# Self-attention of a three-part decoder block: scores and the product with V as plain float32 products on halves of the array

## The chip, the cores and the metric

The kernel runs on one core of one Trainium2 chip. The metric is the time on the device in microseconds (us), the median over runs of the whole program. Engines are named as in the profile: PE is TensorE (matmuls), PEld its weight loads, DVE is VectorE, ACT is ScalarE, POOL is GpSimd, SP is SyncE, which here only issues DMAs.

## The reference

The input x has 16 batches of 128 tokens with 256 features. Three residual blocks follow one another, each on a layernorm of x. Only the first is touched here.

```
x = x + attn(layernorm(x))      # 16 heads of 64, over the 128 tokens of a batch
x = x + xattn(layernorm(x))     # 16 heads of 16, keys and values from ctx, masked
x = x + ffn(layernorm(x))       # 8 experts of 512, gelu, one gate per token

Q, K, V = einsum('btd,hkd->bthk', x, W) + b         # for each of the three
scores  = einsum('bqhk,bshk->bhqs', Q, K) / sqrt(64)
out_h   = einsum('bhqs,bshk->bqhk', softmax(scores), V)
result  = einsum('bqhk,hdk->bqd', out_h, W_O) + b_O
```

## The kernel before

All data are float32. Most matmuls run as three products of values that are split in two parts (`three`, L718): each operand is a rounded high part (type fp32r) and a low part, the rest that rounding left, and high x high, high x low and low x high are summed in PSUM. Every operand that goes into such a product is therefore written twice, mostly the high part by ACT and the low part by DVE or POOL.

The 16 batches form four groups of four (512 tokens). Phase 0 is self-attention of the four groups, phase 1 the cross attention, phase 2 the experts. In phase 0 the 16 heads are taken in 8 chunks of two heads, and each chunk in two slots. A slot holds one "quad": two heads x two batches, four 128x128 score tiles side by side in one PSUM bank (S0 or S1, by turns). 16 slots make a group. Each slot also does one sixteenth of what the group needs beside it: one projection of Q or K for two heads and all 512 tokens (bank A0), one of V for one batch and four heads (left half of bank A1), and half of a chunk's output projection (banks Y0 and Y1). A slot on PE is: scores (L821 to L835), output projection (L893), product with V (`probs_v`, L845), transposes of the probabilities (L841), V projection, Q or K projection.

The life of one quad in phase 0:
- PE: scores from Q (split in two) and K (split in two, laid out with the other head's rows zero, so that one matmul of 256 columns gives two heads), 6 matmuls for two batches.
- DVE: negated row maximum (L1329). ACT: four exponentials with their row sums (L1138). DVE: reciprocal (L1334). POOL: normalise (L1593).
- PE: four transposes into bank T (L841). ACT: the high part of the transposed probabilities (L1149). DVE: the low part (L1224, tile PT).
- PE: product with V. For each of four tiles a matmul of the high probabilities with both parts of V side by side (L860, 128 columns of weights) and one of the low ones with the high part of V (L863, 64 columns). Both parts' results stand in different partitions of bank O.
- ACT: copies one half of O (L1156). DVE: adds both halves and the bias (L1352). POOL: splits the result in high (L1609) and low (L1615). PE: output projection.

The order of the work on each engine is written out in tables, `PE_ORDER`, `ACT_ORDER`, `DVE_ORDER`, `POOL_ORDER` (L511 to L568): for each kind of slot a list of steps with a lag in slots. The product with V, for example, lags two slots behind the scores in phase 0. `steps` (L329) turns a slot's number into the steps' arguments, `run` (L410) walks the table. Engines wait for each other by semaphores only. Each of the banks A0, T and O and each half of A1 has one buffer: what fills it next waits until the last reader is done.

At the seam to phase 1, keys and queries of the cross attention make a round trip by DMA through DRAM (`first_keys`, `first_stack`, `first_queries`) before its first scores (L821, L833). In phase 1 the product with V (L873) is already a plain float32 product: lhs and rhs have type float32, are not split, and four heads stand in four groups of 32 output partitions.

## Time and profile before

| what | value |
|---|---|
| median of 3 runs | 878.22 us (877.76 to 878.98) |
| the profiled execution, its own time | 878.83 us |
| its span, first to last instruction | 877.0 us |
| mean granted TensorE clock | 0.992 |
| busy: PE, PEld, DVE, ACT, POOL | 837.7, 747.4, 536.3, 597.8, 303.6 us |
| phase 0, first to last scores of self-attention | 16.4 to 325.6 us |
| phase 1, first scores to last product with V | 331.7 to 503.4 us |

The busy time of PE counts a matmul from its start to the modelled end of its drain, and neighbours overlap, so a busy PE isn't PE at its peak, and a matmul's own duration isn't what it costs. What a sequence of matmuls costs is read from the distance between the starts of one sequence and of the next. In the timeline, equal instructions in a row are merged into one line with their count, and a bracket at the end says how long the engine stood idle before it and for whom.

### The profile page before, as it was taken

The page shows a single profiled execution, that of the slowest core. Times are in us where ns is not written, and L with a number is a line of the kernel's source. Part 1 is how long each engine was busy: PE and PEld are TensorE (multiplying, and loading weights), DVE is VectorE, ACT ScalarE, POOL GpSimd, SP SyncE. Part 2 cuts the span into 40 slices and gives each one's busy share as a digit, 9 for nine tenths or more (in the row PEclk, how much of TensorE's full clock was granted, in tenths as well). Part 3 has the DMA queues.
Part 4 walks back from the last instruction along what each step waited for, and adds up shares of the span by engine and source line. Part 5 has one row for each costly group of instructions (what it writes and reads, how often), then busy time and mean ns, then how long its engine had stood idle before and what let it go on. Part 6 is the DMA issues. An engine that isn't in the chain of part 4 may idle for free.

```text
span 877.0 us, 17326 instructions
## 1 busy us (share of the span) xinstructions
PE 837.7 (96%) x6043; PEld 747.4 (85%) x6043; DVE 536.3 (61%) x1127; ACT 597.8 (68%) x1724; POOL 303.6 (35%) x350
## 2 busy tenths in 40 slices
PE   8999999999999996889887999999999999999998
PEld 7899989989998985677766689998999999999997
DVE  6898898889889876677767564543233322332223
ACT  5999888888888875878788757654544445444643
POOL 5575656445564665575755520000000000000000
PEclk9999999999999998999999899999999999999999
DMA  6220000000000036565564232300000000000000
GB/s 202 90 62 26 1 1 2 1 1 1 1 25 1 1 71 171 132 159 147 119 157 109 62 95 87 96 1 25 2 1 1 24 0 0 0 25 1 1 1 25
DMA packets 22894, 42.25 MB, mean 48 GB/s; under 512 B 3352, under 2 KB 3872, under 8 KB 22816
## 3 DMA queue, kind: packets, MB, share of 16 engines
q1 hardware_dynamic: 21936, 40.64, 17.5%
q8 instruction: 45, 0.74, 0.4%
q10 hardware_dynamic: 880, 0.60, 0.2%
q14 instruction: 33, 0.27, 0.1%
HBM read 30.35 MB, written 10.49 MB: 47 GB/s over the span
## 4 chain that ended last, share of the span: by engine, by line
PE 75%; DVE 11%; ACT 6%; issue 3%; DMA 2%; POOL 1%; SPq 1%; ACTq 0%; POOLq 0%
PE Y L721 26%; PE A L721 24%; PE S L721 15%; PE T L841 4%; ACT probs L1138 3%; PE O L860 2%; DVE arena L1300 2%; DVE nm L1329 2%; PE O L863 1%; DVE xn L1252 1%; DVE probs L1342 1%; DVE arena L1224 1%; DVE PT L1224 1%; DMA wst<-in_pieces 1%; PE S L821 1%
## 5 line engine op out<-in xcount | busy, mean ns | idle before, releaser
L1224 DVE TENSOR_TENSOR PT<-probs,PT 128x512 fp32r<-128x512 f32 x128 | 89.7, 700 | 227.6 <-ACT PT L1204 227.6
L721 PEld LDWEIGHTS Y<-arena,PT 128*128 128x128 f32 x1536 | 199.9, 191 | 11.4 <-DVE PT L1224 1.4
L721 PE MATMUL Y<-arena,PT 128*128 128x256 f32 x1536 | 203.9, 283 | 0.4
L1138 ACT ACTIVATE probs<-S,nm 128x128 f32<-128x128 f32 x512 | 181.7, 377 | 27.8 <-DVE nm L1329 26.4
L1593 POOL TENSOR_TENSOR probs<-probs,rinv 128x512 f32<-128x512 f32 x128 | 133.0, 1043 | 154.3 <-DVE rinv L1334 154.1
L721 PE MATMUL A<-XT,arena 128*128 128x512 f32 x612 | 160.9, 397 | 1.7 <-DVE arena L1300 0.7
L1204 ACT ACTIVATE PT<-probs 128x512 fp32r<-128x512 f32 x128 | 80.8, 631 | 103.0 <-PE Y L721 102.6
L721 PEld LDWEIGHTS A<-XT,arena 128*128 128x128 f32 x612 | 107.8, 189 | 23.4 <-DVE arena L1300 3.9
L1138 ACT ACTIVATION_READ_ACCUMULATOR probs<-S,nm 128x1 f32 x512 | 110.6, 216 | 0.0
L1329 DVE TENSOR_REDUCE nm<-S 128x4 f32<-128x512 f32 x128 | 87.4, 683 | 30.6 <-PE S L833 18.5
L721 PE MATMUL S<-XT,arena 128*128 128x512 f32 x384 | 99.7, 395 | 0.0
L841 PE MATMUL T<-ident,probs 128*128 128x128 f32 x512 | 80.4, 280 | 16.3 <-DVE probs L1342 14.9
L841 PEld LDWEIGHTS T<-ident,probs 128*128 128x128 f32 x512 | 56.7, 142 | 25.1 <-issue 19.3
L721 PEld LDWEIGHTS S<-XT,arena 128*128 128x128 f32 x384 | 68.0, 189 | 11.4
L1352 DVE SCALAR_TENSOR_TENSOR oraw<-O,bias,opart 64x256 f32<-64x256 f32 x128 | 61.0, 477 | 19.4 <-ACT opart L1156 17.6
L721 PE MATMUL Y<-arena 128*128 128x256 f32 x480 | 71.9, 287 | 0.3 <-POOL arena L1615 0.3
L1173 ACT ACTIVATE probs<-S,bias 128x512 f32<-128x512 f32 x64 | 43.7, 683 | 36.5 <-PE S L721 36.5
L1173 ACT ACTIVATE probs<-A,bias 128x512 f32<-128x512 f32 x64 | 43.7, 684 | 36.6 <-PE A L721 36.5
L1588 POOL TENSOR_TENSOR rstd<-ve,mhalf 128x4 f32<-128x4 f32 x12 | 12.6, 1048 | 158.0 <-DVE ve L1239 158.0
L721 PEld LDWEIGHTS Y<-arena 128*128 128x128 f32 x480 | 64.2, 194 | 1.3 <-POOL arena L1615 1.0
L1615 POOL TENSOR_TENSOR arena<-oraw,arena 128x256 fp32r<-128x256 f32 (+1 forms) x72 | 58.4, 811 | 5.2
L721 PEld LDWEIGHTS S<-arena 128*128 128x128 f32 x384 | 54.3, 189 | 5.7 <-DVE arena L1293 0.6
(137 smaller groups left out, 1375.9 us busy)
## 6 DMA issues: line engine op xcount, KB each, us to landing
wst<-in_pieces SPq DMA_DIRECT2D x43, 256.0 KB, 2.6
stage<-arena SPq DMA_DIRECT2D x32, 256.0 KB, 2.3
arena<-stage SPq DMA_DIRECT2D x51, 128.0 KB, 4.0
arena<-stage SPq DMA_DIRECT2D x21, 256.0 KB, 3.9
craw<-in_ctxT SPq DMA_DIRECT2D x4, 512.0 KB, 4.1
out<-craw SPq DMA_DIRECT2D x8, 256.0 KB, 2.3
xs<-in_x SPq DMA_DIRECT2D x3, 512.0 KB, 4.4
craw<-in_pieces SPq DMA_DIRECT2D x6, 256.0 KB, 2.8
```

What stands on the lines that cost most here:

```text
L721: mm = pe.matmul(acc, lhs[a], rhs[b], start=first and i == 0, stop=last and i == 2, skip_group_check=shared)
L841: mm = pe.transpose(T[:, u * P:(u + 1) * P], probs[:, ring(ph, g, n), u * P:(u + 1) * P], ident[:, :])
L860: pe.matmul(O[:, u * P:(u + 1) * P], v4.rearrange("p s c -> p (s c)"), PT[:, n % 2, 0, u * P:(u + 1) * P], start=True, stop=False, skip_gr ...
L1138: last = act.activation(probs[:, ring(ph, g, n), u * P:(u + 1) * P], S[n % 2][:, u * P:(u + 1) * P], ACT.Exp, bias=nm[:, n % 4, u:u + 1], ...
L1173: act.activation(hid(m), H[m % 4][:, :], ACT.Gelu, bias=bias[:, B1 + m:B1 + m + 1]).then_inc(act_done, 1)
L1204: act.activation(PT[:, m % 2, 0, :], hid(m), ACT.Copy).then_inc(h_hi, 1)
L1224: dve.tensor_tensor(out_, src, hi.bitcast(F32), ALU.subtract).then_inc(sem_, 1)
L1300: last = dve.scalar_tensor_tensor(K[rows_, c % 2, 1, :, h, :], bank[rows_, :].rearrange("p (b c) -> p b c", b=TILES), bias[rows_, BK1 + c: ...
L1329: dve.tensor_reduce(nm[:, n % 4, :], s3, axis=AX.X, op=ALU.max, negate=True).then_inc(maxed, 1)
L1352: last = dve.scalar_tensor_tensor(oraw[h * DH1:(h + 1) * DH1, n % 2, 0:256].rearrange("p (b c) -> p b c", b=2), o4[:, :, h, :], bias[0:DH1 ...
L1593: pool.tensor_tensor(p3, p3, rinv[:, n % 4, :].unsqueeze(2).to_broadcast([P, 4, P]), ALU.mult).then_inc(normed, 1)
L1615: pool.tensor_tensor(to[:, 1, :], raw, to[:, 0, :].bitcast(F32), ALU.subtract).then_inc(o_lo, 1)
```

## The change

Phase 0 only, and with it the order tables.

- Q, K, V and the transposed probabilities aren't split any more. Each is one float32 tile (`qkv`, and `probs` in place), written by one engine: K and V by ACT, Q by DVE, the transposed probabilities of even quads by ACT, of odd ones by DVE.
- Both slots of a chunk are scored in one go (`chunk_scores`): for four batches and two heads, 8 plain float32 matmuls of 128x128 with 64 rows of contraction. Head 0 stands in partitions 0 to 63 of Q and K and goes to bank S0, head 1 in partitions 64 to 127 and goes to S1.
- The product with V of a chunk is in one go too (`chunk_v`): 8 plain float32 matmuls, head 0 into partitions 0 to 63 of bank O, head 1 into 64 to 127.
- The result is taken from O by DVE in two instructions, high part with bias and low part with bias, straight into `AT`. ACT's copy, DVE's two sums and POOL's two splits of phase 0 go.
- The tables have new steps "even", "odd" and "cross". In phase 0 scores and product with V come once per two slots; transposes lag one quad, the product with V one chunk. A quad index now stands for one head and four batches. An evacuation of Q, K or V stands in the slot of its projection, not in the next one.
- The cross attention's tiles KP, QP, XA and the second context buffer have places of their own in the arena, so several waits at the seam go (in `split_context`, `blank_keys`, `qk_evac`, `part_hi`). `scores` and `probs_v` for phase 1 compute what they did.

```diff
...
-        V = region(4096).rearrange("p (r t h s c) -> p r t h s c", r=2, t=TILES, h=4, s=2)
-        K = region(4096).rearrange("p (r s b h c) -> p r s b h c", r=2, s=2, b=TILES, h=2)
-        Q = region(2048).rearrange("p (r s c) -> p r s c", r=2, s=2)
+        def halves_of(what, cols):
+            return cols.rearrange(f"p (s {what} t) -> p s {what} t", s=2, t=GT)
+        CT = [halves_of("k", region(2048)), halves_of("k", region(2048))]
+        XA = halves_of("k", region(2048))
+        KP = region(2048).rearrange("p (r s c) -> p r s c", r=2, s=2)
+        QP = region(2048).rearrange("p (r s c) -> p r s c", r=2, s=2)
         AT = region(2048).rearrange("p (r s c) -> p r s c", r=2, s=2)
...
+        qkv = sb("qkv", [P, 4096], F32)
+        V = qkv[:, 0:2048].rearrange("p (r t h c) -> p r t h c", r=2, t=TILES, h=4)
+        K = qkv[:, 2048:3072].rearrange("p (r c) -> p r c", r=2)
+        Q = qkv[:, 3072:4096].rearrange("p (r c) -> p r c", r=2)
...
-                return XT if g % 2 else CT[0]
+                return XT if g % 2 else PT
...
         PE_ORDER = (
-            (("scores", "quad", (0, 0)), ("proj", "proj", (4, 6)),
-             ("pv", "quad", (2, 5)), ("transpose", "quad", (1, 3)), ("xp", "xp", (0, 0)),
-             ("v", "v", (0, 0)), ("qk", "qk", (0, 0))),
+            (("xp", "xp", (0, 0)), ("v", "v", (0, 0)), ("transpose", "odd", (1, 0)), ("qk", "qk", (0, 0)),
+             ("scores", "even", (0, 0)), ("pv", "odd", (1, 0)), ("transpose", "even", (1, 0)),
+             ("proj", "proj", (3, 6))),
...
+            def chunk_scores(g, c):
+                pe.wait_ge(qk_lo, nth(QK_F1, 0, g, 2 * c + 1))
+                pe.wait_ge(exped, nth(SLOT_F2, 0, g, 2 * c - 1))
+                for b in range(TILES):
+                    at = slice(b * P, (b + 1) * P)
+                    for h in range(2):
+                        rows_ = slice(h * DH1, (h + 1) * DH1)
+                        mm = pe.matmul(S[h][:, at], Q[rows_, c % 2, at], K[rows_, c % 2, at],
+                                       start=True, stop=True)
+                        if b == TILES - 1:
+                            mm.then_inc(scores_ps, 1)
...
-                        b, h = 2 * (n % 2) + u // 2, u % 2
-                        v4 = V[:, cp % 2, b, 2 * (c % 2) + h, :, :]
-                        pe.matmul(O[:, u * P:(u + 1) * P], v4.rearrange("p s c -> p (s c)"),
-                                  PT[:, n % 2, 0, u * P:(u + 1) * P], start=True, stop=False,
-                                  skip_group_check=True)
-                        mm = pe.matmul(O[0:DH1, u * P:(u + 1) * P], v4[:, 0, :],
-                                       PT[:, n % 2, 1, u * P:(u + 1) * P], start=False, stop=True,
-                                       skip_group_check=True)
...
+            def chunk_v(g, c):
+                if c % 2 == 0:
+                    pe.wait_ge(v_lo, nth(VJ_F1, 0, g, 2 * c + 3))
+                pe.wait_ge(o_lo, nth(SPLIT_F2, 0, g, c - 1))
+                for b in range(TILES):
+                    for h in range(2):
+                        mm = pe.matmul(O[h * DH1:(h + 1) * DH1, b * P:(b + 1) * P],
+                                       V[:, c // 2 % 2, b, 2 * (c % 2) + h, :],
+                                       probs[:, ring(0, g, 2 * c + h), b * P:(b + 1) * P],
+                                       start=True, stop=True)
+                        if b == TILES - 1:
+                            mm.then_inc(pv_ps, 1)
...
+                    c = job // 2
+                    act.wait_ge(qk_ps, nth(QK, ph, g, job))
+                    act.activation(K[:, c % 2, :], bank_qk(ph, g, job)[:, :], ACT.Identity,
+                                   bias=bias[:, BK1 + c:BK1 + c + 1]).then_inc(qk_lo, 1)
+                    return
...
-            def probs_hi(ph, g, n):
-                if ph == 1 and n % 2 == 0:
-                    return
-                act.wait_ge(pt_ps, nth(SLOT_F4, ph, g, n))
-                if ph == 0:
-                    act.wait_ge(pv_ps, nth(SLOT_F2, ph, g, n - 2))
-                    act.activation(PT[:, n % 2, 0, :], T[:, :], ACT.Copy).then_inc(pt_hi, 1)
-                else:
+            def probs_copy(ph, g, n):
+                if ph == 0 or n % 2 == 1:
+                    act.wait_ge(pt_ps, nth(SLOT_F4, ph, g, n))
                     act.activation(probs[:, ring(ph, g, n), :], T[:, :], ACT.Copy).then_inc(pt_lo, 1)
-            def out_first(ph, g, n):
-                if ph == 0:
-                    act.wait_ge(pv_ps, nth(SLOT_F2, ph, g, n))
-                    act.activation(opart[DH1:P, :], O[DH1:P, :], ACT.Copy).then_inc(o_part, 1)
...
             def qk_low(ph, g, job):
+                    if job == 1 and opening(g):
+                        dve.wait_ge(ready_b, 2)
+                    c = job // 2
+                    dve.wait_ge(qk_ps, nth(QK, ph, g, job))
+                    dve.tensor_scalar(Q[:, c % 2, :], bank_qk(ph, g, job)[:, :], bias[:, BQ1 + c:BQ1 + c + 1],
+                                      None, ALU.add).then_inc(qk_lo, 1)
+                    return
...
-            def v_low(ph, g, job):
-                if ph == 0:
-                    dve.wait_ge(v_hi, nth(VJ, ph, g, 3 if opening(g) and job == 2 else job))
-                    r, t = job // 4 % 2, job % 4
-                    sub_lo(V[:, r, t, :, 1, :], acc_v(g, job).rearrange("p (h c) -> p h c", h=4),
-                           V[:, r, t, :, 0, :], v_lo)
...
+            def row_max(ph, g, quad):
+                for n in (quad, quad + 1) if ph == 0 else (quad,):
+                    dve.wait_ge(scores_ps, nth(SLOT, ph, g, n))
+                    s3 = S[n % 2][:, :].rearrange("p (u c) -> p u c", u=4)
+                    dve.tensor_reduce(nm[:, n % 4, :], s3, axis=AX.X, op=ALU.max, negate=True
+                                      ).then_inc(maxed, 1)
...
             def out_sum(ph, g, n):
-                c = n // 2
                 if ph == 0:
-                    dve.wait_ge(o_part, nth(PART, ph, g, n))
-                    dve.wait_ge(o_lo, nth(SPLIT_F2, ph, g, n - 2))
-                    o4 = O[0:DH1, :].rearrange("p (b h c) -> p b h c", b=2, h=2)
-                    p4 = opart[DH1:P, :].rearrange("p (b h c) -> p b h c", b=2, h=2)
-                    for h in range(2):
-                        last = dve.scalar_tensor_tensor(
-                            oraw[h * DH1:(h + 1) * DH1, n % 2, 0:256].rearrange("p (b c) -> p b c", b=2),
-                            o4[:, :, h, :], bias[0:DH1, BV1 + 2 * c + h:BV1 + 2 * c + h + 1],
-                            p4[:, :, h, :], ALU.add, ALU.add)
-                    last.then_inc(o_sum, 1)
+                    c = n // 2
+                    dve.wait_ge(pv_ps, nth(SLOT_F2, ph, g, n))
+                    dve.wait_ge(oproj, nth(OPROJ, ph, g, c - 2))
+                    dve.tensor_scalar(AT[:, c % 2, 0, :], O[:, :], bias[:, BV1 + c:BV1 + c + 1],
+                                      None, ALU.add).then_inc(o_hi, 1)
...
+            def out_low(ph, g, n):
+                c = n // 2
+                dve.wait_ge(o_hi, nth(SPLIT, ph, g, c))
+                dve.scalar_tensor_tensor(AT[:, c % 2, 1, :], O[:, :], bias[:, BV1 + c:BV1 + c + 1],
+                                         AT[:, c % 2, 0, :].bitcast(F32), ALU.add, ALU.subtract
+                                         ).then_inc(o_lo, 1)
...
```

PE in the middle of a group, before: two slots (one chunk's worth), from one Q or K projection to the next chunk's. T is the bank of the transposes, A those of the projections, S the scores, Y the output projection, O the product with V.

```order
L721 MATMUL A<-XT,arena 128x512 x6
L721 MATMUL S<-arena 128x256 x6
L721 MATMUL Y<-arena 128x256 x6
L860 MATMUL O<-PT,arena 128x128
L863 MATMUL O<-PT,arena 64x128
...
L841 MATMUL T<-ident,probs 128x128 x4
L721 MATMUL A<-arena,XT 128x256 x6
```

The rows for O stand four times each, then the slot begins again. Now the same engine in the middle of a group, one chunk:

```order
L838 MATMUL S<-qkv 128x128 x8
L881 MATMUL O<-probs,qkv 64x128 x8
L720 MATMUL Y<-arena 128x256 x6
L720 MATMUL A<-arena,XT 128x256 x6
L720 MATMUL A<-XT,arena 128x512 x6
L847 MATMUL T<-ident,probs 128x128 x4
L720 MATMUL Y<-arena 128x256 x6
L720 MATMUL A<-arena,XT 128x256 x6
L847 MATMUL T<-ident,probs 128x128 x4
L720 MATMUL A<-XT,arena 128x512 x6
```

Scores and product with V now stand side by side once per chunk, and the two transposes of a chunk stand behind and ahead of the Q or K projections. ACT before, one slot of each kind (`probs` the exponentials, `opart` the copy of O, `PT` the high probabilities, `arena<-A` the high parts of V, Q and K):

```order
L1138 ACTIVATE probs,rsum<-S,nm 128x128 x4
L1156 ACTIVATE opart<-O 64x512
L1149 ACTIVATE PT<-T 128x512
L1118 ACTIVATE arena<-A 128x4x64
L1101 ACTIVATE arena<-A,bias 64x4x128 x2
L1138 ACTIVATE probs,rsum<-S,nm 128x128 x4
...
L1118 ACTIVATE arena<-A 128x4x64
L1096 ACTIVATE arena<-A,bias 128x512
```

ACT now, one chunk:

```order
L1127 ACTIVATE probs,rsum<-S,nm 128x128 x8
L1109 ACTIVATE qkv<-A 128x256
L1085 ACTIVATE qkv<-A,bias 128x512
L1136 ACTIVATE probs<-T 128x512
L1109 ACTIVATE qkv<-A 128x256
```

The eight exponentials of a chunk stand together; V, K and one copy of transposed probabilities follow.

## Rows read from the trace of the kernel before

**Rows 1.** The page: busy time by engine; chain that ended last, by engine.
```profile
PE 837.7 (96%) x6043; PEld 747.4 (85%) x6043; DVE 536.3 (61%) x1127; ACT 597.8 (68%) x1724; POOL 303.6 (35%) x350
PE 75%; DVE 11%; ACT 6%; issue 3%; DMA 2%; POOL 1%; SPq 1%; ACTq 0%; POOLq 0%
```

**Rows 2.** Windows: stretch, then busy us of each engine, PEclk, DMA share, GB/s.
```profile
100.00:150.00 50.00, 49.24 (x379) 45.65 (x378) 44.55 (x96) 42.18 (x133) 28.92 (x37) 1.00 0.01 1
300.00:350.00 50.00, 42.11 (x295) 38.47 (x294) 35.47 (x74) 33.84 (x120) 31.58 (x36) 0.93 0.44 106
```

**Rows 3.** Timeline of PE, two slots, and token transposes (L928): start, length (us), operation.
```profile
253.51 1.66 PE L721 MATMUL A<-XT,arena 128*128 128x512 f32 x6
255.00 0.87 PE L721 MATMUL S<-arena 128*128 128x256 f32 x6
255.71 0.88 PE L721 MATMUL Y<-arena 128*128 128x256 f32 x6
256.43 0.22 PE L860 MATMUL O<-PT,arena 128*128 128x128 f32 x1
...
257.06 0.63 PE L841 MATMUL T<-ident,probs 128*128 128x128 f32 x4
257.44 0.96 PE L721 MATMUL A<-arena,XT 128*128 128x256 f32 x6
258.24 1.53 PE L721 MATMUL A<-XT,arena 128*128 128x512 f32 x6
259.61 0.88 PE L721 MATMUL S<-arena 128*128 128x256 f32 x6
...
301.33 0.38 PE L928 MATMUL A<-ident,xn 128*128 128x128 f32 x2
301.47 0.96 PE L721 MATMUL A<-arena,XT 128*128 128x256 f32 x6
```

**Rows 4.** Timeline of PE: the same wait in two neighbouring groups, and another one.
```profile
156.37 1.64 PE L721 MATMUL A<-XT,arena 128*128 128x512 f32 x6 [0.34 <-DVE arena L1300]
234.50 1.64 PE L721 MATMUL A<-CT,arena 128*128 128x512 f32 x6 [0.34 <-DVE arena L1300]
267.82 0.98 PE L721 MATMUL A<-arena,XT 128*128 128x256 f32 x6 [0.61 <-DVE arena L1224]
```

**Rows 5.** Timeline of PE in phase 1: plain float32 products (L873) between others.
```profile
413.32 0.60 PE L841 MATMUL T<-ident,probs 128*128 128x128 f32 x4
413.85 0.65 PE L873 MATMUL O<-probs,wst 128*32 128x128 f32 x16
414.43 0.50 PE L821 MATMUL S<-dropped,identr 128*128 128x512 f32 x1
```

**Rows 6.** Timeline of PE, short stretches of such a product: its first four records; the last twelve.
```profile
404.25 0.32 PE L873 MATMUL O<-probs,wst 128*32 128x128 f32 x4
...
404.39 0.51 PE L873 MATMUL O<-probs,wst 128*32 128x128 f32 x12
```

**Rows 7.** Line 873, 400 to 410 us: duration of a record, ns, shortest, median, longest.
```profile
L873 PE MATMUL O<-probs,wst x48: 272/273/297, 399.8 to 409.4; 128*32 128x128 f32 x48
```

**Rows 8.** Timeline of DVE, ACT and POOL: one quad from maximum to evacuations.
```profile
255.91 0.69 DVE L1329 TENSOR_REDUCE nm<-S 128x4 f32<-128x512 f32 x1 [0.32 <-PE S L721]
256.64 0.37 ACT L1138 ACTIVATE probs<-S,nm 128x128 f32<-128x128 f32 x1 [0.74 <-DVE nm L1329]
257.93 0.21 ACT L1138 ACTIVATION_READ_ACCUMULATOR probs<-S,nm 128x1 f32 x1
258.18 0.18 DVE L1334 RECIPROCAL rinv<-rsum 128x4 f32<-128x4 f32 x1 [0.58 <-ACT probs L1138]
258.43 1.04 POOL L1593 TENSOR_TENSOR probs<-probs,rinv 128x512 f32<-128x512 f32 x1 [0.91 <-DVE rinv L1334]
258.79 0.60 ACT L1149 ACTIVATE PT<-T 128x512 fp32r<-128x512 f32 x1
259.28 0.38 ACT L1118 ACTIVATE arena<-A 128x256 fp32r<-128x256 f32 x1
```

**Rows 9.** Groups of instructions by line and form, 100 to 300 us: busy, mean ns.
```profile
L1293 DVE SCALAR_TENSOR_TENSOR arena<-A,bias,arena 128x512 fp32r<-128x512 f32 x21 | 15.6, 741 | 0.0
L1372 DVE TENSOR_TENSOR xs<-Y,xs 128x512 f32<-128x512 f32 x6 | 3.9, 686 | 0.1
L1588 POOL TENSOR_TENSOR rstd<-ve,mhalf 128x4 f32<-128x4 f32 x3 | 3.1, 1018 | 4.4 <-DVE ve L1239 4.4
```

**Rows 10.** Timeline: ACT's K in one piece, at the seam.
```profile
318.40 0.69 ACT L1107 ACTIVATE arena<-A,bias 128x512 fp32r<-128x512 f32 x1
```

**Rows 11.** Timeline of PE at the seam from self-attention to cross attention.
```profile
316.56 1.65 PE L721 MATMUL A<-CT,arena 128*128 128x512 f32 x6
...
331.71 0.77 PE L821 MATMUL S<-dropped,identr 128*128 128x512 f32 x1 [2.85 <-DMA arena<-arena]
...
349.90 0.94 PE L721 MATMUL A<-arena 128*128 128x512 f32 x3 [1.64 <-issue]
...
351.21 0.64 PE L873 MATMUL O<-probs,wst 128*32 128x128 f32 x16
```

340 lines of the change are left out of this document (130 added, 210 removed), and 2 rows, old and new, of the table PE_ORDER.

## Prediction

> **What bounds the kernel now.** First the page, for the engine that sets the end: PE's share of the chain that ended last is 75%, and of the 877.0 us it is busy for 837.7 [rows 1]. The windows show that this isn't an average over unlike stages: in the middle of phase 0 PE is busy for 49.24 of 50 us at full clock (2.4 GHz, PEclk 1.00), while DVE, ACT and POOL have 5 to 21 us to spare; only the seam to phase 1 has a hole, 42.11 of 50 us, with the mean clock at 0.93 [rows 2]. The reader is to see there that phase 0, which is all that changes, costs what PE's list of instructions costs. So the next view is PE's timeline, read from start to start. A slot is: scores 0.71 us (255.00 to 255.71), output projection 0.72, product with V 0.63, transposes 0.38, V 0.80, Q or K 1.37; together 4.61 [rows 3]. Two slots, one chunk's worth, are 9.22 us of pure PE work. The same wait one group later gives the true pace: 234.50 - 156.37 = 78.13 us for 8 such pairs, 9.77 us a pair [rows 4]. So 0.55 us a pair is not this work: waits for DVE, which writes the low parts (0.34 for K in one slot, 0.61 for V beside the residual) [rows 4], a second Q or K projection that takes 1.49 in place of 1.37 [rows 3], and the next group's token transposes, 4 a group at 0.14 [rows 3], or 0.07 a pair.
>
> **The change, part by part.**
>
> *PE, removed.* Per pair two times 0.71 for scores and 0.63 for the product with V, 2.68 us. What stays is 2 x (0.72 + 0.38 + 0.80 + 1.37) = 6.54 us.
>
> *PE, added.* 8 plain float32 products for scores and 8 with V per chunk. Phase 1 has such products, with four heads in four groups of 32 output partitions. Eight products (two quads, four heads) show as 16 records [rows 5], so one product is two passes. The first four records take 0.32 us from first start to last end where one takes up to 0.297 [rows 6, 7], so four start within 0.02 us and run side by side. From the second four to the last start is 0.51 - 0.27 = 0.24 us, less that spread 0.22 for two steps: 0.11 us a step of 128 columns. 16 records in pairs are 8 steps, 0.88 us, for the product with V, where two output halves stand side by side, and I take the same for scores, where two row halves do. No row shows two row halves. The bounds: 0.88 us if they run side by side with their weight loads as the output groups do, 16 x 0.12 = 1.92 us if each record costs what one of the present scores does (0.71 / 6) [rows 3]. I take 0.88, because the nearest row is the plain product, whose neighbours don't wait for one another in weights or matmuls. Below 0.88 there is no reason: a step has to stream its 128 columns twice.
>
> Then the passage between shapes: the four transposes at 413.32 take 0.38, but the product starts 0.53 us after them, so entry costs 0.15; its 4 steps take 0.44 of the 0.58 us to the next matmul, so exit costs 0.14 [rows 5]. A chunk has three passages (into scores, from there to the product with V, out): 0.15 + 0.15 + 0.14 = 0.44. The trace shows what TensorEngine Tiling of the Trainium skill (section Key Properties) states, that a change of tiling mode drains the engine; without that drain the sum would be 14 us lower (32 x 0.44), and I keep the rows.
>
> A pair is now 6.54 + 2 x 0.88 + 0.44 = 8.74 us, plus 0.07 for token transposes: 8.81.
>
> *ACT.* Per chunk it loses one of two copies from T (0.60), two copies of O and the Q part, and keeps eight exponentials (256.64 to 258.14, 1.50 us for four), two V copies of 0.38, one K of 0.69 and one copy of 0.60 [rows 8, 10]: 5.1 of 8.8 us. *DVE:* two maxima, one copy, Q, two results, each 0.69 to 0.74 [rows 8, 9], two reciprocals of 0.18: 4.6 us. *POOL:* two normalisations of 1.04 [rows 8]. All lie beside PE. The splits that go cost nothing where PE did not wait for them; where it did, the waits on K low and V low go with them, about 0.4 of the 0.55 us a pair.
>
> *What is late next.* The lag shrinks, so the chain of a chunk must be laid beside PE's list. From the end of scores: PE 1.17 (passages and product with V) + 0.72 + 0.80 + 1.37 = 4.06, then T of head 0. Its probabilities are ready at 0.04 + 0.69 maximum + 1.50 exponentials + 0.18 + 1.04 + 0.2 for the hand-overs = 3.7 [rows 8]. Hidden by 0.4. T of head 1 comes at 4.06 + 0.38 + 0.72 + 0.80 = 5.96. Head 1's normalisation ends at 3.7 + 1.50 = 5.2, but bank T is free only once ACT has copied head 0, behind four more exponentials (3.8), V and K: K ends at about 4.95, the copy at 5.6. Hidden by 0.35. So PE keeps the pace, barely. What stands on DVE and POOL once a group breaks through: the reciprocal root (1.02 [rows 9]) now stands ahead of a head-1 normalisation, some 0.9 us late; the residual (2 x 0.69 [rows 9]) ahead of a head-1 reciprocal, some 0.6; the context splits and weight splits on POOL and ACT a few tenths each. I take 2 us a group, 0.25 a pair. A pair becomes 9.06.
>
> *Seam.* Cross projections to cross scores take 331.71 - 316.56 = 15.15 us now, 2.85 of them idle, for data by DMA [rows 11]. In the new order PE has some 16 us of its own work there (chunk 7 whole, four projection pairs, two products with V), so that DMA hides, and behind the first cross scores only two output projections are left of self-attention instead of three products with V and four projections. The stretch up to 351.21, 34.7 us, is then bound by exponentials and by the idle 1.64 for data at 349.90 [rows 11], so that I count 2 us gained, from 0 to 5. Opening: same work, and 1 us lost where a weight's rounding stands ahead of the K copy.
>
> *Sum.* 32 pairs x (9.77 - 9.06) = 22.7; seam 2; opening -1: 23.7 us less. Against the profiled execution's own 878.83 that is 855.1; the median is 0.6 lower, 854.5 us.
>
> **Rivals.**
>
> A. *The chain takes over.* The slack is 0.35 us a pair, and hand-overs are estimates from gaps of 0.04 to 0.07. If the chain is 0.8 longer, the pace is 0.45 longer a pair: 854.5 + 14 = 869. For: S0 and S1 are both used by a chunk, so nothing of the next one can be scored ahead. Against: every term is a measured row.
>
> B. *Row halves don't load side by side* (the other side). Each of the 16 records of scores has 128 columns of weights, where the rows above have 32, and 32-column loads are too short to show whether they wait for one another. If they go one after another at 0.12, scores take 1.92 in place of 0.88. The chain then hides better, so that stalls fall from 0.25 to 0.1: the pair is 8.81 + 1.04 + 0.1 = 9.95, 0.18 more than now, 32 x 0.18 = 6 us slower, less 1 for the seam: 883. It decides from 0.10 us a record, where scores reach 1.6. TensorE: Matmul & The Clock Gate of the Trainium skill (Part 3) says that weight loads overlap running matmuls only where the row group differs. By that rule row halves are the good case and the product with V, on column halves, the bad one: its loads of 64 columns would come on top, by the page's figure (columns / 1.2, ns) an estimated 0.05 us for each of 8 steps, 14 us in all. The time would be 868. The rows disagree, since four column groups with all rows in common make a step in 0.11 with loads included [rows 6, 7], so it gets a chance of 0.02.
>
> C. *No two halves run side by side at all.* 16 x 0.11 = 1.76 for each: the pair is 10.57, 0.8 more than now, 904. Rows 6 speak against it for outputs.
>
> D. *More hides than I think.* No new stalls and a good seam: 32 x 0.25 and 3 more, 843.
>
> **Chances.** Forecast 0.62 (848 to 862), A 0.11, column halves one after another by loads 0.02, B 0.12, C 0.03, D 0.10. What the measurement can tell from no change is 0.2%, 1.8 us. Faster holds the forecast, A, the column case and D, 0.85. Of B, 0.04 with cheaper loads is no change; the rest of B and C, 0.11, is slower. The range reaches from below D's 843 to beyond A; B's 883 is left out but for its cheap part: 841 to 879.
>
> **What would show it.** In the new profile: scores to product with V 1.03 us apart on PE (0.88 and a passage), product to output projection 1.02; 2.1 in place of 1.0 for the scores is B. Pairs of 8.8 to 9.1 us, with transposes of head 1 at most 0.2 us late in most of them; if they wait for ACT's copy or POOL in each pair, it is A. No wait for DVE ahead of a projection. First cross scores without an idle gap for DMA. The prediction is wrong if the pair isn't below 9.4 us, or if the clock falls below 2.4 GHz inside phase 0.

## The result, and the profile after

The changed kernel takes 866.52 us (median of 4 runs, 865.48 to 867.98); the kernel before took 878.03 us beside it (4 runs, 877.76 to 878.98). The ratio is 0.9868, interval 0.985 to 0.9886: 11.5 us less, where 23.7 were forecast. The direction was right, and the size less than half of it. The profiled execution took 867.98 us, with a span of 866.2, against 877.0 before.

The page of the changed kernel, the two lines that answer to [rows 1]:

```profile
PE 822.1 (95%) x6171; PEld 713.3 (82%) x6171; DVE 438.4 (51%) x903; ACT 491.9 (57%) x1564; POOL 227.7 (26%) x221
PE 76%; DVE 8%; ACT 6%; POOL 5%; issue 4%; DMA 0%; SPq 0%; ACTq 0%; POOLq 0%; DVEq 0%
```

POOL works a quarter less than before, and yet its share of the chain has gone from 1% to 5%: it is now waited for. DMA has left the chain. The windows, to be read beside [rows 2], with two short stretches of their own:

```profile
55.00:60.00 5.00, 4.64 (x22) 4.05 (x24) 1.47 (x4) 0.66 (x2) 1.43 (x2) 0.66 0.29 105
100.00:150.00 50.00, 47.89 (x404) 41.31 (x403) 30.20 (x61) 27.66 (x116) 18.94 (x17) 1.00 0.00 1
320.00:326.00 6.00, 4.46 (x26) 4.33 (x28) 0.69 (x1) 0.15 (x1) 4.96 (x4) 0.72 0.71 240
```

In the middle of phase 0 PE is busy for 47.89 of 50 us, where it was 49.24, though DVE, ACT and POOL all have less to do than before. And there are two stretches at a low mean clock: 0.66 in the opening group from 55 to 60 us, 0.72 at the seam from 320 to 326.

PE's timeline over one undisturbed pair (it answers to [rows 3]; L838 are the scores of a chunk, L881 its product with V):

```profile
153.34 1.16 PE L838 MATMUL S<-qkv 64*128 64x128 f32 x16
154.43 1.09 PE L881 MATMUL O<-probs,qkv 128*64 128x128 f32 x16
155.46 0.97 PE L720 MATMUL Y<-arena 128*128 128x256 f32 x6
...
162.16 1.05 PE L838 MATMUL S<-qkv 64*128 64x128 f32 x14
```

From scores to scores it is 162.16 - 153.34 = 8.82 us; scores to product with V 1.09, product with V to output projection 1.03. The forecast had 1.03, 1.02 and 8.74 (8.81 with the mean share of token transposes). What PE has to do in a pair was forecast to 0.1 us.

So the loss must stand between such pairs. The starts of scores of the second group lie, one pair after the other, 8.83, 9.00, 9.82, 10.60, 9.30, 9.54, 8.82 and 8.83 us apart, 74.74 in all (96.25 to 170.99), where a group took 78.13 [rows 4]. Two views show what the long ones hold. PE's waits, from 11 to 335 us, most of the way through the seam (in total, times, longest):

```profile
PE T L847 <- POOL probs L1553: 7.2, 10, 2.1
PE A L933 <- DVE xn L1232: 6.2, 4, 2.2
```

And the timeline of two places, one for the third pair of a group (9.82), one for the fourth (10.60):

```profile
119.84 1.02 POOL L1548 TENSOR_TENSOR rstd<-ve,mhalf 128x4 f32<-128x4 f32 x1 [1.00 <-DVE ve L1219]
120.83 1.04 POOL L1553 TENSOR_TENSOR probs<-probs,rinv 128x512 f32<-128x512 f32 x1
121.92 0.66 PE L847 MATMUL T<-ident,probs 128*128 128x128 f32 x4 [0.77 <-POOL probs L1553]
...
127.61 1.04 POOL L1553 TENSOR_TENSOR probs<-probs,rinv 128x512 f32<-128x512 f32 x1 [5.75 <-DVE rinv L1297]
128.09 2.01 DVE L1232 TENSOR_SCALAR xn<-xs,mv,rstd 128x256 f32<-128x256 f32 x2
128.61 1.33 POOL L1581 TENSOR_TENSOR xs<-xs,rowc 128x512 f32<-128x512 f32 x1
130.10 1.43 DVE L1232 TENSOR_SCALAR xn<-xs,mv,rstd 128x256 f32<-128x256 f32 x2
130.26 1.12 POOL L1553 TENSOR_TENSOR probs<-probs,rinv 128x512 f32<-128x512 f32 x1 [0.32 <-DVE rinv L1297]
131.59 0.44 PE L933 MATMUL A<-ident,xn 128*128 128x128 f32 x2 [1.33 <-DVE xn L1232]
```

First place: the reciprocal root (`rstd`) stands on POOL ahead of head 1's normalisation, and the transposes of head 1 come about 1 us late. This one was in the forecast (0.9). Second place: DVE applies the layernorm (xn) to four tiles while POOL normalises, adds the output bias, and normalises again. The first two xn take 2.01 us together, the next two 1.43, where one takes 0.40 to 0.42 with POOL idle, and PE, which wants to transpose xn, waits 1.33 us. That is in no term of the forecast. Taken singly, the second and the fourth:

```profile
128.72 1.37 DVE L1232 TENSOR_SCALAR xn<-xs,mv,rstd 128x256 f32<-128x256 f32 x1
...
130.40 1.13 DVE L1232 TENSOR_SCALAR xn<-xs,mv,rstd 128x256 f32<-128x256 f32 x1
```

The groups of DVE by form, 40 to 300 us (busy us, mean ns), before and after:

```profile
L1252 DVE TENSOR_SCALAR xn<-xs,mv,rstd 128x256 f32<-128x256 f32 x16 | 7.6, 513 | 0.1
```
```profile
L1232 DVE TENSOR_SCALAR xn<-xs,mv,rstd 128x256 f32<-128x256 f32 x16 | 14.6, 953 | 0.0
```

The same operation on the same shape takes nearly twice as long. In the opening group the weight splits stand on POOL too, and the wait is the longest (timeline of PE):

```profile
55.36 0.69 PE L933 MATMUL A<-ident,xn 128*128 128x128 f32 x2 [2.22 <-DVE xn L1232]
55.70 1.63 PE L720 MATMUL A<-arena,PT 128*128 128x256 f32 x6
```

Behind 2.22 idle us the V projection takes 1.63 instead of 0.88: PE is at the lower of its two levels, 1.2 GHz, for part of the stretch whose mean is 0.66, which costs another 0.34 x 5 = 1.7 us. The same happens at the seam (it answers to [rows 11]):

```profile
319.22 1.26 POOL L1603 TENSOR_TENSOR arena<-craw,arena 128x512 fp32r<-128x512 f32 x1
320.44 1.04 POOL L1553 TENSOR_TENSOR probs<-probs,rinv 128x512 f32<-128x512 f32 x1
321.54 1.11 PE L847 MATMUL T<-ident,probs 128*128 128x128 f32 x4 [2.08 <-POOL probs L1553]
...
326.76 0.50 PE L819 MATMUL S<-dropped,identr 128*128 128x512 f32 x1
...
338.13 1.32 PE L720 MATMUL A<-arena 128*128 128x512 f32 x3 [1.64 <-issue]
340.24 1.08 PE L868 MATMUL O<-probs,wst 128*32 128x128 f32 x16
```

The first cross scores (326.76) wait for no DMA any more, as forecast. But 5 us ahead of them PE is idle for 2.08 us, since the context's split stands on POOL ahead of the last normalisation. The first product of phase 1 comes at 340.24 instead of 351.21 [rows 11], 10.97 us earlier, and that is the whole gain of the profiled executions: from there to the end the kernels take 525.83 us before and 525.94 after.

The clock at the seam needs care, for the kernel before ran at the lower level there as well, behind its wait for DMA. The same stretch, from the last chunk's scores to the first product of phase 1, before and after:

```profile
319.41:351.20 31.79, 24.36 (x162) 22.05 (x160) 20.64 (x45) 17.94 (x69) 19.20 (x23) 0.89 0.71 168
```
```profile
312.97:340.24 27.27, 19.79 (x145) 16.75 (x144) 17.10 (x37) 14.43 (x69) 14.32 (x13) 0.91 0.83 173
```

By these means the clock costs at most 0.11 x 31.79 = 3.5 us before and 0.09 x 27.27 = 2.5 after, less where PE has to wait anyway. At the seam it is no new loss of the changed kernel.

Where these 10.97 us arise needs one correction, for the stretches from scores to scores don't hold the same work before and after. In the stretch of the opening group PE now has one output projection, one V projection, one Q or K projection and four transposes more, and as much less later on, nearly all of it at the seam. The output projections in the opening stretch, before (16.37 to 93.82) and after (15.84 to 96.24), show the shift, 6 matmuls; at the seam there are 36 before and 30 after:

```profile
L721 PE MATMUL Y<-arena 128*128 128x256 f32 x72 | 10.6, 283 | 0.0
```
```profile
L720 PE MATMUL Y<-arena 128*128 128x256 f32 x78 | 12.6, 297 | 0.3 <-POOL arena L1540 0.3
```

| stretch | before, us | after, us | less, us | less, at equal work | forecast |
|---|---|---|---|---|---|
| to the first scores | 16.38 | 15.85 | 0.5 | 0.5 | 0 |
| opening group | 77.45 | 80.40 | -2.9 | 0.3 | 4.7 |
| second group | 78.13 | 74.74 | 3.4 | 3.4 | 5.7 |
| third group | 78.14 | 74.24 | 3.9 | 3.9 | 5.7 |
| fourth, 7 pairs | 69.32 | 67.75 | 1.6 | 2.3 | 5.0 |
| last chunk to first product of phase 1 | 31.79 | 27.26 | 4.5 | 0.6 | 2.7 |

(The work that moved, an output projection, a V projection, a Q or K projection and four transposes, is about 3.3 us; the fourth group has one Q or K projection more and one V projection less, 0.7; the seam has 3.9 less. The forecast column is 0.71 a pair, with the opening's -1 and the seam's 2 and one pair.)

### The profile page after: what moved, and what is told of

Its sections match the earlier page's. It is cut to its first block, busy times and chain, and to the rows that moved or that the text cites. A ratio compares the mean times of both kernels' runs of the same rounds, so it can differ in the third digit from the quotient of the medians.

```text
span 866.2 us, 16891 instructions
## 1 busy us (share of the span) xinstructions
PE 822.1 (95%) x6171; PEld 713.3 (82%) x6171; DVE 438.4 (51%) x903; ACT 491.9 (57%) x1564; POOL 227.7 (26%) x221
## 4 chain that ended last, share of the span: by engine, by line
PE 76%; DVE 8%; ACT 6%; POOL 5%; issue 4%; DMA 0%; SPq 0%; ACTq 0%; POOLq 0%; DVEq 0%
PE Y L720 25%; PE A L720 23%; PE S L720 10%; PE T L847 5%; ACT probs L1127 5%; PE S L838 4%; PE O L881 3%; POOL probs L1553 2%; DVE xn L1232 2%; DVE probs L1302 1%; PE S L949 1%; PE S L819 1%; POOL rstd L1548 1%; ACT arena L1099 1%; PE O L868 1%
## 5 line engine op out<-in xcount | busy, mean ns | idle before, releaser
L1127 ACT ACTIVATION_READ_ACCUMULATOR probs<-S,nm 128x1 f32 x512 | 113.8, 222 | 0.0
L1292 DVE TENSOR_REDUCE nm<-S 128x4 f32<-128x512 f32 x128 | 84.6, 682 | 28.1 <-PE S L826 16.1
L847 PEld LDWEIGHTS T<-ident,probs 128*128 128x128 f32 x512 | 60.8, 144 | 39.1 <-issue 19.5
L1302 DVE COPY probs<-T 128x512 f32<-128x512 f32 x64 | 44.0, 687 | 75.8 <-PE T L847 75.8
L720 PE MATMUL Y<-arena 128*128 128x256 f32 x480 | 76.6, 296 | 1.1 <-DVE arena L1321 0.5
L1136 ACT ACTIVATE probs<-T 128x512 f32<-128x512 f32 x64 | 38.6, 603 | 33.8 <-PE T L847 33.8
L720 PE MATMUL A<-PT,arena 128*128 128x512 f32 x174 | 46.7, 403 | 0.1
```

What stands on the lines that cost most here:

```text
L720: mm = pe.matmul(acc, lhs[a], rhs[b], start=first and i == 0, stop=last and i == 2, skip_group_check=shared)
L847: mm = pe.transpose(T[:, u * P:(u + 1) * P], probs[:, ring(ph, g, n), u * P:(u + 1) * P], ident[:, :])
L1127: last = act.activation(probs[:, ring(ph, g, n), u * P:(u + 1) * P], S[n % 2][:, u * P:(u + 1) * P], ACT.Exp, bias=nm[:, n % 4, u:u + 1], ...
L1136: act.activation(probs[:, ring(ph, g, n), :], T[:, :], ACT.Copy).then_inc(pt_lo, 1)
L1292: dve.tensor_reduce(nm[:, n % 4, :], s3, axis=AX.X, op=ALU.max, negate=True).then_inc(maxed, 1)
L1302: dve.tensor_copy(probs[:, ring(ph, g, n), :], T[:, :]).then_inc(pt_lo, 1)
```

## The experiments

Eleven changed versions of the changed kernel were run, and the kernel before beside each batch of them took 877.8 to 878.2 us. Runs of one kernel spread by some 2 to 6 us, so that a difference of 1 to 2 us between two medians isn't told apart; the traces are finer, and in the middle groups a pair that nothing has touched repeats within 0.05 us. Two theories stood against each other. T1: DVE's xn is long because POOL works beside it, and PE waits for it; the reciprocal root and the context split ahead of a normalisation are the rest. T2: those waits are only where a chain that is too long shows itself, so that moving one of them makes another (the forecast's rival A). The expectations of runs 1 and 3 call the view that the waits are the loss T, and the view that another wait takes their place R.

**1. Layernorm one chunk earlier.**

```diff
+        STATS_PARTED = {-8: ALL[:2], -7: ALL[2:]}
-        NORM_PARTED = {-3: ALL[:2], -2: ALL[2:]}
+        NORM_PARTED = {-5: ALL[:2], -4: ALL[2:]}
...
-                tiles = {"stats": STATS1[1], "norm": NORM_PARTED, "aggr": {AGGR1[1]: None}}[name]
+                tiles = {"stats": STATS_PARTED, "norm": NORM_PARTED, "aggr": {AGGR1[1] - 2: None}}[name]
```

Expected: 

> The layernorm of the next group (statistics, aggregate, reciprocal root, application) stands one chunk earlier in the tables; nothing else changes. Theory T (the missing gain is idle time of PE that the layernorm's place on DVE and POOL causes): the wait of the first token transposes for DVE's xn, 6.2 us in 4 places, and the stretch at half clock behind the first of them (about 1.3 us) go; the wait for the normalisation behind the reciprocal root stays at 0.8 us a group. 866.5 becomes 859 to 860. Rival theory R (the row and column halves cost more than read from the trace of before, the waits are covered by something else that is late as well): the wait moves to another instruction and the time stays within 2 us of 866.5.

Measured: 866.15 us (864.87 to 867.36), ratio 0.9867 (0.9843 to 0.9892), no gain over the change itself that can be told. PE's waits, 11 to 335 us:

```profile
PE T L848 <- POOL probs L1554: 12.1, 10, 2.2
```

The wait for xn (6.2) is gone, and the wait for POOL has grown by most of that, from 7.2 to 12.1 us. The timeline of DVE, POOL and PE shows by which way: one chunk earlier the statistics stand right behind the residual, the root comes late, and the second normalisation stands behind the root.

```profile
109.88 0.16 DVE L1298 RECIPROCAL rinv<-rsum 128x4 f32<-128x4 f32 x1
110.78 1.02 POOL L1549 TENSOR_TENSOR rstd<-ve,mhalf 128x4 f32<-128x4 f32 x1 [2.19 <-DVE ve L1220]
111.77 1.04 POOL L1554 TENSOR_TENSOR probs<-probs,rinv 128x512 f32<-128x512 f32 x1
112.87 0.66 PE L848 MATMUL T<-ident,probs 128*128 128x128 f32 x4 [1.79 <-POOL probs L1554]
```

The reciprocal is done at 110.04, the normalisation starts at 111.77. The second pair of a group takes 11.01 us, the fourth 9.06. By its median this run looks like T2. The trace is milder: a middle group takes 0.5 us less, the stretch at 1.2 GHz from 55 us is gone, and from the first to the last scores of self-attention it takes 294.74 us in place of 297.13, 2.4 less. The expected 6.5 to 7.5 us are missed all the same.

**2. Output bias two slots later on POOL.**

```diff
-        BIAS_AT = (14, 17)
+        BIAS_AT = (16, 17)
```

Expected: 

> POOL's addition of the output bias (1.3 us a half, two halves a group) stands two slots later for its first half, away from DVE's application of the layernorm. Theory T1 (DVE's xn takes 1.12 us in place of 0.41 because POOL works on SBUF at the same time): the first two xn of a group fall from 2.0 us together to about 1.3, the wait of PE behind them from 1.3 to about 0.4 us a group, 4 to 5 us less in all with the clock, 862. Rival T2 (xn is only placed too late, its length has nothing to do with POOL): xn stays at 1.1 us, the time at 866.

Measured: 861.02 us (860.24 to 862.99), ratio 0.9809 (0.9783 to 0.9835), 5.5 us less than the change. The add is the same, 1.33 us long, only not beside xn. The four xn of the second group took 0.72, 1.37, 0.38 and 1.13 us in the changed kernel, and take 0.72, 0.40, 0.38 and 1.13 now: the one that ran beside the add has fallen, the two beside normalisations stay. DVE's timeline, to be read beside 2.01 and 1.43 above, then PE's waits:

```profile
125.53 1.04 DVE L1232 TENSOR_SCALAR xn<-xs,mv,rstd 128x256 f32<-128x256 f32 x2
...
126.58 1.43 DVE L1232 TENSOR_SCALAR xn<-xs,mv,rstd 128x256 f32<-128x256 f32 x2
```
```profile
PE A L933 <- DVE xn L1232: 2.5, 4, 1.4
```

The wait for xn is 2.5 in place of 6.2 us, and the one for POOL is unchanged at 7.2: nothing came back elsewhere. In the opening group the fourth pair takes 10.61 instead of 12.96, 2.35 less. Only 0.8 of it is the shorter wait (1.4 for 2.2); the rest is the clock, which stays at 1.00 between 55 and 60 us. T1 holds here.

**3. The root behind the second normalisation.**

```diff
-             ("bias", "bias", (3, 6)), ("aggr", "aggr", (0, 0)),
+             ("bias", "bias", (3, 6)), ("aggr", "aggr", (1, 0)),
```

Expected: 

> POOL's reciprocal root for the next group stands behind, not ahead of, the normalisation of the same chunk's second head, in phase 0. Theory T: the wait of the transposes for POOL loses 0.8 us in each of three groups and 1.15 in the opening one, 3 to 3.5 us less, 863; if the root then comes too late for DVE's xn, the wait for xn grows by at most 0.3 a group. Rival R: no change beyond 1 us.

Measured: 865.1 us (863.75 to 866.33), ratio 0.9858 (0.9833 to 0.9882). The median is 1.4 us less, within the runs' spread, and less than expected; the profile has the effect without doubt (PE's waits):

```profile
PE T L847 <- POOL probs L1553: 4.5, 7, 2.1
```

7.2 has become 4.5, and the third pair 8.83 in place of 9.82 in the second and third group. From the first to the last scores of self-attention the trace has 293.87 us in place of 297.13, 3.3 less, as expected. Its seam then takes 28.02 us in place of 27.26, at a mean clock of 0.83 in place of 0.91.

**4. Scores in turn.** Head 0's four products first, then head 1's, so that two row halves don't alternate.

```diff
-                for b in range(TILES):
-                    at = slice(b * P, (b + 1) * P)
-                    for h in range(2):
+                for h in range(2):
+                    for b in range(TILES):
+                        at = slice(b * P, (b + 1) * P)
```

Expected: 

> The 8 score products of a chunk come head by head (four of row half 0, then four of row half 1), so that no two neighbours stand in different row halves, except at the one change. Same products. If neighbours in different row halves run side by side in the changed kernel (theory H), scores take about 16 x 0.11 = 1.8 us a chunk in place of 0.9, and 32 chunks add 25 to 29 us: 892 to 895. If the halves' weight loads or matmuls are in turn anyway (rival), the order makes no difference: 866.

Measured: 875.32 us (874.41 to 878.39), ratio 0.9972 (0.9959 to 0.9985). PE's timeline:

```profile
164.75 1.71 PE L838 MATMUL S<-qkv 64*128 64x128 f32 x16
166.39 1.09 PE L881 MATMUL O<-probs,qkv 128*64 128x128 f32 x16
```

Scores to product with V is 1.64 in place of 1.09 us. So the halves did run side by side, which the forecast took without a row for two row halves; its rival B is out. The cost of taking them in turn was expected too high: not 8 steps of 0.11 more but 5, 0.55 us, as the first records of head 1 start before the last of head 0 are through. Then the pair is 9.38, and 32 times 0.55 would be 17.6 us; measured are 8.8, half of it. PE's longer list hides part of the waits, 7.9 us in place of 13.4, and PE stays at 1.00 behind the shorter one in the opening:

```profile
PE A L933 <- DVE xn L1232: 4.1, 4, 1.7
PE T L847 <- POOL probs L1553: 3.8, 6, 2.1
```

**5. Product with V in turn.** The same swap of the two loops in `chunk_v`.

```diff
-                for b in range(TILES):
-                    for h in range(2):
+                for h in range(2):
+                    for b in range(TILES):
```

Expected: 

> The eight products with V of a chunk are issued head by head, so that no two column halves of the output stand next to each other in PE's list, except where head 0 gives way to head 1. If column halves run side by side as row halves did (scores in turn took 1.71 us in place of 1.16, 13 steps of 0.11 in place of 8), the product with V takes 0.5 to 0.6 us longer, the pair 9.3 to 9.4 instead of 8.83, and with the waits shrinking as they did there the kernel ends at 873 to 878 us. If the halves of the output are not run side by side now (the rival: the load of one half waits for the other half's matmul), the order makes no difference and the time stays at 866.5.

Measured: 874.93 us (872.51 to 878.91), ratio 0.9961 (0.9946 to 0.9975), and in PE's timeline

```profile
164.34 1.58 PE L881 MATMUL O<-probs,qkv 128*64 128x128 f32 x16
165.85 0.98 PE L720 MATMUL Y<-arena 128*128 128x256 f32 x6
```

1.51 us to the output projection in place of 1.03; the pair is 9.32. Column halves run side by side as row halves do. By the rule of TensorE: Matmul & The Clock Gate of the Trainium skill (Part 3), that weight loads overlap running matmuls only where the row group differs, the loads of column halves, whose rows are all in common, should come on top of the matmuls: an estimated 0.05 us for each of 8 steps, by the page's figure for loads. The trace doesn't agree: a step takes 0.11 us with its loads, and the product with V takes 1.03 us, as the rows without such a term gave it.

**6. Context split one slot later at the seam.**

```diff
-                    return [(g + 1, part) for part in {10: (0, 1, 2), 15: (3,)}.get(v, ())]
+                    return [(g + 1, part) for part in {11: (0, 1, 2), 15: (3,)}.get(v, ())]
```

Expected: 

> At the seam the split of the context's first three parts is issued one slot later (11 instead of 10), so that it no longer stands on POOL ahead of the normalisation that the last transposes wait for. Theory: the idle 2.08 us of PE at 321.54 is gone, and with it the stretch at half clock right behind it; 2 to 3.5 us less, 863 to 864.5 us. Rival: the time at the seam is set by the exponentials and by data, and the wait only moves to behind 326: 866.5.

Measured: 862.56 us (860.1 to 863.96), ratio 0.9819 (0.9804 to 0.9834), 4 us less than the change. PE's timeline at the seam:

```profile
320.30 0.63 PE L847 MATMUL T<-ident,probs 128*128 128x128 f32 x4
...
321.48 1.60 PE L720 MATMUL A<-arena 128*128 128x256 f32 x12
```

The last transposes wait for nothing, and the twelve matmuls behind them take 1.60 us in place of 2.08. From 320 to 326 us the mean clock is 1.00 here, where it was 0.72. In the changed kernel the idle 2.08 us came with another 0.28 x 6 = 1.7 at 1.2 GHz, 3.8 together. The whole stretch to the first product of phase 1 takes 22.94 us in place of 27.26, 4.3 less: in this trace the second drop of the clock, behind the wait at 338.13, is missing too. That the clock holds when this wait is gone isn't sure: the split is moved in runs 7 to 9 as well, and their seams run at a mean of 0.86 to 0.93, lowered at other places.

**7. Three moves together (2, 3 and 6).**

Expected: 

> Output bias on POOL two slots later, the reciprocal root behind the second normalisation, context split one slot later, together. Each takes a different wait of PE away: 5.5, 1.4 and 2 to 3.5 us by themselves. If they are independent the sum is 9 to 10.5: 856 to 857.5 us, with third pairs of a group near 9.6 and the fourth at 8.83. If POOL's work only moves from one wait to another, as it did when the layernorm went a chunk earlier, at most the best of them is left: 861 us.

Measured: 854.38 us (852.42 to 857.43), ratio 0.973 (0.9717 to 0.9743). That is 12.1 us less than the change; the three alone gave 5.5 + 1.4 + 4.0 = 10.9, and 9 to 10.5 were expected. The traces add up more closely. From the first to the last scores of self-attention the change takes 297.13 us, run 2 291.89, run 3 293.87 and this one 288.56: 5.2 and 3.3 less alone, 8.6 together. So the waits aren't one long chain that shows in several places. This decides against T2 and rival A.

**8. Four moves (1, 2, 3 and 6).**

Expected: 

> The three moves together with the layernorm one chunk earlier. By itself the last bought nothing, as its root then stood ahead of the normalisation and its statistics beside the residual. With the root behind the normalisation the waits for xn (2.5 us left after the bias move) go, and the waits for the normalisation stay as without it: 854 to 856 us. Rival: the statistics beside the residual delay the reciprocals all the same, which gives back 4 to 5 us: 858 to 861 us.

Measured: 854.6 us (853.88 to 855.81), ratio 0.9737 (0.9725 to 0.975), the same as with three. In the middle groups it is better: the second takes 72.56 us against 72.82. But the root of the group that opens phase 1 is ordered by another lag of the table, still stands ahead of a normalisation, and costs one pair 12.48 us. PE's timeline:

```profile
254.75 0.96 PE L848 MATMUL T<-ident,probs 128*128 128x128 f32 x4 [1.79 <-POOL probs L1554]
255.37 2.91 PE L721 MATMUL A<-XT,arena 128*128 128x512 f32 x6
```

After 1.79 idle us the Q or K projection takes 2.91 instead of 1.64 us: another place where PE falls to the lower level. In run 1 the transposes waited equally long, 1.79 us at 112.87, and the pair took 11.01: there it didn't fall, nor behind 2.17 idle us at 36.22. A wait of this length can do it and need not.

**9. All roots behind, with four moves and with three.**

```diff
-             ("bias", "bias", (3, 6)), ("aggr", "aggr", (1, 0)),
+             ("bias", "bias", (3, 6)), ("aggr", "aggr", (1, 1)),
```

Expected, on top of four: 

> The four moves, and the reciprocal root behind the normalisation for the group that opens the next phase too. In the run with four moves that one root still stood ahead of a normalisation: the transposes waited 1.79 us, a stretch at half clock followed, and the pair took 12.48 us in place of about 9.4. If that wait starts the slow stretch, both go and 3 us are gained: 851 to 852 us. If the seam has slack anyway, the time stays at 854.6.

Measured: 853.22 us (852.73 to 854.71), ratio 0.9726 (0.9713 to 0.9739). The pair of 12.48 takes 9.36, and the last chunk's scores come 3.2 us earlier. The medians show 1.4 us of that, within the spread. In the traces the first product of phase 1 comes 2.6 us earlier and the end 2.2, so that most of it gets through; the seam's mean clock is 0.87 in place of 0.93. Whether the seam has slack isn't shown.

Expected, on top of three: 

> The three moves, with the same change for the last root. There the pair with the root took 9.82 in place of 8.83 us, so that 1 us should go: 853.4 us, and less than 1 if the seam has slack.

Measured: 855.72 us (852.28 to 857.71), ratio 0.9739 (0.9718 to 0.976), no difference to run 7 that can be told. In the trace the pair went from 9.82 to 8.83, and the first product of phase 1 comes 1.4 us earlier than in run 7 (327.91 and 329.35); the medians, 1.3 us apart the other way, don't show it.

**10. A narrow bias add.** POOL's add in the place of the changed kernel, with its semaphores, on 16 of 256 columns of a tile; the other 240 get no bias.

```diff
+                w = D if ph else 16
-                add = pool.tensor_tensor(dst, dst, rowc[:, ph * D:(ph + 1) * D].unsqueeze(1)
-                                         .to_broadcast([P, 2, D]), ALU.add)
+                add = pool.tensor_tensor(dst[:, :, 0:w], dst[:, :, 0:w],
+                                         rowc[:, ph * D:ph * D + w].unsqueeze(1)
+                                         .to_broadcast([P, 2, w]), ALU.add)
```

Expected: 

> In the changed kernel POOL adds the output bias of phase 0 to 16 columns of a tile instead of 256 (the bias of the other columns is left out): same place in POOL's list, same semaphores, a fraction of the time. If the layernorm on DVE is slow because POOL works beside it, the applications that ran beside the add (1.37 and 1.13) fall to about 0.4 where no normalisation is beside them, PE's wait for xn shrinks from 1.3 to under 0.5 us a group and from 2.2 to under 1 in the opening, the slow stretch behind it goes, and the time is 860 to 862 us, as with the add moved. Rival: they are slow for their place in DVE's list (hand-overs between its own instructions and PE's banks): durations and 866.5 us stay.

Measured: 861.9 us (860.72 to 862.37), ratio 0.9818 (0.9805 to 0.9831), as with the add moved. Timeline of POOL and DVE:

```profile
126.07 1.04 DVE L1232 TENSOR_SCALAR xn<-xs,mv,rstd 128x256 f32<-128x256 f32 x2
126.59 0.30 POOL L1582 TENSOR_TENSOR xs<-xs,rowc 128x32 f32<-128x32 f32 x1
```

The add takes 0.30 us, the first two xn 1.04 instead of 2.01, the next two, beside a normalisation as before, 1.43; nothing was reordered. From the first to the last scores it takes 291.85 us, where run 2 took 291.89. It is POOL's work beside them, not their place in DVE's list. In the opening PE still waits 1.3 us for xn (under 1 was expected), as normalisations and a weight split stay on POOL there.

## Why the forecast had the direction and missed the size

**Right: PE's list.** Eight steps of 0.11 for scores, taken without a row for two row halves, 1.09 us with passage where 1.03 was forecast; product with V 1.03 for 1.02; the undisturbed pair 8.83 against 8.74. Runs 4 and 5 show that both depend on the halves standing side by side. Small as they are, these sizes add up: 0.09 for each of 31 pairs is 2.8 us, and a token transpose costs 0.235 in place of 0.14, 1.5 us for 16 of them. That is 4.3 of the 12.2 us that the forecast missed. The other 8 are waits of PE and clock.

**Right: the base slack of the chain.** Undisturbed pairs have no wait at all, with copies and normalisations in the order that the forecast laid out. Rival A names a time of 869, near the measured one, but not by its mechanism: it wants a wait in each pair, and eight of the 31 distances take 8.82 to 8.84 us, the sum of PE's instructions.

**Right: K low, V low and DMA.** No projection waits for a low part any more, and no first cross scores for DMA.

**Wrong: "I take 2 us a group, 0.25 a pair" for what is late next.** The second group's 74.74 us are 8 x 8.83 = 70.64, four token transposes at (9.30 - 8.83) / 2 = 0.235, 0.94, and 3.2 of stalls: xn 1.5, the root 1.0, and 0.7 in two late normalisations, 0.2 behind the residual and 0.5 behind a memset of `wst` that holds POOL for 1.81 us (from 148.49). Against the forecast of 9.06 x 8 = 72.5 that is 2.3 us too much: stalls 1.2, the pair 0.7, token transposes 0.4. What was priced (the root 0.9) was right; the residual, behind which a reciprocal should make the transposes 0.6 late, makes them 0.2 late (the pair of 9.00); and neither xn nor the memset was in the list at all. The step that failed is the one by which the list was made: it took each operation at its duration in the old order and asked only who stands ahead of whom on one engine. The application of the layernorm, 0.51 us on the mean before, got no term. In the new order it lies beside three operations of POOL, and it takes 0.95 us. The trace of before held the hint: in the opening group, beside a weight split on POOL (52.31 to 53.66), an xn took as long.

```profile
52.43 1.38 DVE L1252 TENSOR_SCALAR xn<-xs,mv,rstd 128x256 f32<-128x256 f32 x1
```

**Wrong: "Opening: same work, and 1 us lost".** It kept 0.3 us of a forecast gain of 4.7 at equal work. The waits for POOL and xn come to 3.9 us there, since weight splits stand on POOL as well, and PE ran from 55 to 60 us at a mean clock of 0.66, which is another 1.7. The forecast named a clock below 2.4 GHz inside phase 0 as a sign that it was wrong; it was seen.

**Wrong: "I count 2 us gained" at the seam.** The 2.85 us for DMA went, but 2.08 for POOL came, and at equal work 0.6 us were gained of 2.7. The forecast had no term for the clock, neither for the 3.5 us at most that it cost there before nor for the 2.5 after. Run 6, without the wait for POOL and at full clock, takes 22.94 us, 4.3 less than the change.

Together the three moves of run 7 take 12 us off and land at 854.4, where the forecast was. It had forecast about the kernel that the change could be, with POOL's side work out of the way. That the numbers meet so closely is luck: run 7 has the dearer pair and token transposes, and makes up for them by fewer stalls than were forecast, 1.2 in place of 2 us in the second group (72.82 - 70.64 - 0.94).

Open: why the waits of 1.79 us at 112.87 (run 1) and at 254.75 (run 8), alike in length, left the clock alone in one and lowered it in the other, and why the seam's mean clock differs from run to run, 0.83 to 1.00. Neither was tried by itself.

## What to carry to other kernels

When a change moves work of one engine to another place, price it again by what the other engines do beside it there, not by its duration in the old place; look above all for DVE operations between SBUF tiles that come beside POOL. Once PE has no slack, one instruction of 1 us that is rare and stands ahead of a frequent one on POOL is worth moving behind it, and such moves add up. Where medians of runs spread by more than a small effect, compare the distances in the traces, stretch by stretch. An idle stretch of PE of 2 us can cost twice its length by the clock, so the longest waits go first.

## What the runs showed of the hardware

- DVE's 128x256 float32 operation from SBUF to SBUF takes 0.40 to 0.42 us alone, 0.38 where POOL's instruction starts behind it, and 0.58 to 1.38 where one of POOL that lasts 1 us or more is already running. It is the same beside POOL's add to xs, its normalisation of probs and its weight split, so that it doesn't hang on a tile in common. The ends tell how: in the changed kernel the second xn runs from 128.72 to 130.10, and POOL's add from 128.61 to 129.94; the fourth from 130.40 to 131.53, and POOL's normalisation from 130.26 to 131.38. DVE finishes 0.15 us behind POOL in both. SBUF — State Buffer of the Trainium skill (section Who interferes with whom) says that DVE in its two-port modes and POOL share a pair of ports under an exclusive lock, held for a whole instruction. The trace agrees: the DVE instruction that starts second ends behind POOL's, whatever its own length. That xn runs in such a mode no run shows by itself.
- POOL is held up as well, though by less: the normalisation that starts at 130.26, beside a third xn begun at 130.10, takes 1.12 in place of 1.04 us.
- Two halves of PE's array, by rows or by columns, take one step of 0.11 us for two records, one of each half; a plain float32 matmul of 128 columns is two records. In turn they take 0.55 and 0.48 us more per 16 records.
- Idle stretches of PE of 2.08 to 2.85 us in work that is otherwise dense came with the lower clock level in 11 of the 12 places where the traces have one up to the seam's end; behind 2.17 us at 36.22 (run 1) the clock stayed. Of six of 1.70 to 1.80 us one did, that of run 8.
